# The bias of the folded linear layers: added to every row by GpSimd, or by a small matmul for each bin

## The reference, cut to what matters

```python
def gnn(x, edge_row, edge_col, W1, b1, W2, b2):
    agg = jax.ops.segment_sum(x[edge_col], edge_row, num_segments=6250)
    h = agg + x
    return (h @ W1 + b1) @ W2 + b2

x = x + gnn(layernorm(x), src, dst, ...)        # x: 6250 x 256, 100000 edges
x = x + experts(layernorm(x)[None], ...)[0]     # 8 experts, three layers each, weighted by a softmax
```

## Time and profile before

| | |
|---|---|
| median of 3 runs | 1579.49 us (1576.08 to 1580.27) |
| profiled execution | 1576.09 us, its span 1574.3 us |
| busy | PE 1236.1 us, DVE 1258.2, ACT 884.8, POOL 983.9 |
| first gather issued | 311.07 us from the span's start |
| last gather issued | 1410.40 us |

### The profile page before, as it was taken

One profiled execution on the slowest core, in us unless ns is written; L12 is line 12 of the kernel. 1 busy time (PEld: TensorE's weight loads), 2 busy tenths in 40 slices (PEclk: granted clock), 3 DMA queues, 4 the chain that ended last, 5 costly groups with the idle time before them and its releaser, 6 DMA issues.

```text
span 1574.3 us, 27908 instructions
## 1 busy us (share of the span) xinstructions
PE 1236.1 (79%) x7858; PEld 777.2 (49%) x7858; DVE 1258.2 (80%) x3421; ACT 884.8 (56%) x1593; POOL 983.9 (63%) x1001
## 2 busy tenths in 40 slices
PE   0035443554579999998999989999899999989996
PEld 0035332421235556565565656556565665645565
DVE  7999999864477888887888878988788888875655
ACT  6976656000054656665565655656556565656877
POOL 1140799177777777777777777777777777760000
PEclk9977655665699999999999999999999999999999
DMA  8020244043333343433434344343433434361000
GB/s 239 1 80 11 94 137 140 6 130 105 104 103 103 103 128 102 131 105 103 128 101 131 99 117 118 100 128 103 131 102 102 128 99 127 99 83 34 18 1 17
DMA packets 84072, 153.23 MB, mean 97 GB/s; under 512 B 18151, under 2 KB 56330, under 8 KB 83908
## 3 DMA queue, kind: packets, MB, share of 16 engines
q0 software_dynamic: 40608, 110.94, 25.5%
q1 hardware_dynamic: 43300, 40.36, 8.1%
HBM read 131.97 MB, written 19.27 MB: 96 GB/s over the span
## 4 chain that ended last, share of the span: by engine, by line
PE 45%; DVE 31%; issue 10%; DMA 6%; POOL 3%; DVEq 2%; ACT 2%; POOLq 0%; ACTq 0%; SPq 0%
PE PB L1318 10%; PE PA L1303 10%; PE PL L1335 9%; DVE zz L664 7%; DVE zz L665 6%; PE PN L1234 6%; DMA gbuf<-xn_hilo,dsti 6%; DVE acc L917 5%; PE PN L1235 4%; POOL gbuf L423 3%; DVE onehot L847 3%; PE PT L1259 3%; DVE xt L1023 1%; DVEq L900 1%; DVE zz L768 1%
## 5 line engine op out<-in xcount | busy, mean ns | idle before, releaser
L423 POOL DMA_INDIRECT gbuf<-xn_hilo,dsti x846 | 842.8, 996 | 291.2 <-issue 180.7
L917 DVE TENSOR_TENSOR acc<-acc,PN 128x256 f32 x798 | 331.6, 416 | 169.8 <-PE PN L1235 155.8
L1303 PE MATMUL PA<-yT,wsplit 128*128 128x512 f16 (+1 forms) x1248 | 290.8, 372 | 11.8 <-issue 11.8
L1335 PE MATMUL PL<-wsplit,h 128*128 128x256 f16 x2352 | 289.5, 273 | 11.3 <-DVE h L1008 4.2
L1318 PE MATMUL PB<-h,wsplit 128*128 128x512 f16 (+1 forms) x1248 | 284.7, 367 | 0.0
L557 ACT ACTIVATE h<-PA,bnt,bns 128x512 f16<-128x512 f32 (+1 forms) x208 | 156.6, 753 | 225.5 <-PE PA L1303 219.4
L1234 PE MATMUL PN<-gbuf,onehot 128*128 128x256 f16 x798 | 209.3, 283 | 83.5 <-DVE acc L917 44.7
L571 ACT ACTIVATE h<-PB,bnt,bns 128x512 f16<-128x512 f32 (+1 forms) x208 | 156.4, 752 | 203.9 <-PE PB L1318 199.5
L1335 PEld LDWEIGHTS PL<-wsplit,h 128*128 128x128 f16 x2352 | 227.9, 98 | 47.3 <-ACT zz L572 10.5
L1235 PE MATMUL PN<-gbuf,onehot 128*128 128x256 f16 x798 | 208.4, 282 | 0.0
L1234 PEld LDWEIGHTS PN<-gbuf,onehot 128*128 128x128 f16 x798 | 78.3, 98 | 233.9 <-DVE acc L917 122.1
(11 more groups left out here) (214 smaller groups left out, 1222.7 us busy)
## 6 DMA issues: line engine op xcount, KB each, us to landing
gbuf<-xn_hilo,dsti POOLq DMA_INDIRECT x846, 2.8
x_plus_bias<-xst SPq DMA_DIRECT2D x49, 128.0 KB, 1.7
xn_hilo<-onehot SPq DMA_DIRECT2D x49, 128.0 KB, 1.7
xt<-x_plus_bias SPq DMA_DIRECT2D x49, 128.0 KB
out<-xt SPq DMA_DIRECT2D x49, 128.0 KB
acc<-in_x SPq DMA_DIRECT2D x4, 1536.0 KB
h<-in_L_ffn_W SPq DMA_DIRECT2D x16, 256.0 KB, 2.8
h<-in_L_ffn_Wo SPq DMA_DIRECT2D x8, 256.0 KB, 2.7
```

Of the source, the lines that this page charges most:

```text
L423: pool.indirect_dma_start(gbuf[:, k % SLOTS, :], None, xn_dram, bass.IndirectOffsetOnAxis(dsti[:, k:k + 1], 0)).then_inc(gat[k % SLOTS], 16)
L917: V.tensor_tensor(to, to, bank[:, i, :], ALU.add).then_inc(s["acc_done"], 1)
L1303: last = T_.matmul(PA[:, h, 0:w], wsp[0][:, e, k, wp, h * P:(h + 1) * P], yT[:, par, yp, k, 0:w], start=n == 0, stop=n == 5)
L1335: last = T_.matmul(PL[:, i % 2, :], h2[:, e % 2, yp, k, i * P:(i + 1) * P], wsp[2][:, e, k, wp, :], start=n == 0, stop=n == 5)
```

## The change

x itself is stored to DRAM (`x_whole_bins`), by five transfers out of `acc` right after x is in, ahead of the loads of the layers' weights on SyncE's queue. The additions of b12 on GpSimd and the 49 stores of their results are gone; ScalarE's loop no longer waits for them, only once for the five stores. The bias is split into three f16 parts, one in each of three rows of `b3`, by six small instructions on ScalarE and GpSimd, with waits between them, and `linear` adds it to each bin's PSUM by a matmul of a 3-row `ones3` with `b3`. The loops of SyncE and GpSimd over the bins lose their lag of three.

```diff
+            sp.wait_ge(s["x_in"], 16 * 5)
+            for c in range(4):
+                sp.dma_start(x_dram[12 * c * P:(12 * c + 12) * P, :].rearrange("(t p) d -> p t d", p=P),
+                             acc[:, 12 * c:12 * c + 12, :]).then_inc(s["x_stored"], 16)
+            sp.dma_start(x_dram[(BINS - 1) * P:NPAD, :], acc[:, BINS - 1, :]).then_inc(s["x_stored"], 16)
             sp.dma_start(gw1, gW1.rearrange("(k p) n -> p k n", p=P)).then_inc(s["gnnw_in"], 16)
...
-            for t in range(BINS + LN_LAG):
-                if t < BINS:
-                    sp.wait_ge(s["xb_ready"], t + 1)
-                    sp.dma_start(xb_dram[t * P:(t + 1) * P, :], xst[:, t % 2, :]).then_inc(
-                        s["xst_stored" if t % 2 == 0 else "xst_stored1"], 16)
-                if t >= LN_LAG:
-                    u = t - LN_LAG
-                    sp.wait_ge(s["xnhi_ready"], u + 1)
-                    sp.wait_ge(s["xnlo_ready"], u + 1)
-                    sp.dma_start(xn_dram[u * P:(u + 1) * P, :], nst[:, u % 4, :]).then_inc(s[f"nst_stored{u % 4}"], 16)
+            for t in range(BINS):
+                sp.wait_ge(s["xnhi_ready"], t + 1)
+                sp.wait_ge(s["xnlo_ready"], t + 1)
+                sp.dma_start(xn_dram[t * P:(t + 1) * P, :], nst[:, t % 4, :]).then_inc(s[f"nst_stored{t % 4}"], 16)
...
+            pool.memset(ones3[:], 1.0).then_inc(s["b3_const"], 1)
+            for i in range(2):
+                pool.tensor_scalar(b3r[:, i:i + 1], bcol[0:3, :], i + 0.5, None, ALU.is_gt).then_inc(s["b3_const"], 1)
...
-            pool.wait_ge(s["b12_ready"], 1)
-            for t in range(BINS + LN_LAG):
-                if t < BINS:
-                    if t >= 2:
-                        pool.wait_ge(s["xst_stored" if t % 2 == 0 else "xst_stored1"], 16 * (t // 2))
-                    pool.tensor_tensor(xst[:, t % 2, :], acc[:, t, :], b12[:], ALU.add).then_inc(s["xb_ready"], 1)
...
+            pool.wait_ge(s["b3_high"], 1)
+            pool.tensor_tensor(b3w[:], b12[0:3, :], b3m[:], ALU.subtract).then_inc(s["b3_rest"], 1)
...
+            for t in range(BINS):
+                pool.wait_ge(s["xnhi_ready"], t + 1)
+                pool.tensor_tensor(nst[:, t % 4, D:2 * D], acc[:, t, :], nst[:, t % 4, 0:D],
+                                   ALU.subtract).then_inc(s["xnlo_ready"], 1)
             weights_low(range(W_FIRST, NW))
+            pool.wait_ge(s["b3_high"], 2)
+            pool.tensor_tensor(b3w[:], b3w[:], b3m[:], ALU.subtract).then_inc(s["b3_rest"], 1)
...
             nc.scalar.activation(b12[:], PL[:, 0, :], ACT.Copy).then_inc(s["b12_ready"], 1)
+            act.wait_ge(s["b12_ready"], 1)
+            act.wait_ge(s["b3_const"], 3)
+
+            def b3_high(values, i):
+                nc.scalar.activation(b3[:], values, ACT.Copy).then_inc(s["b3_part"], 1)
+                act.wait_ge(s["b3_part"], i + 1)
+                nc.scalar.activation(b3m[:], b3[:], ACT.Copy, scale=b3r[:, i:i + 1]).then_inc(s["b3_high"], 1)
+
+            b3_high(b12[0:3, :], 0)
...
+            act.wait_ge(s["b3_rest"], 1)
+            b3_high(b3w[:], 1)
             act.wait_ge(s["xnm_ready"], 1)
+            act.wait_ge(s["x_stored"], 16 * 5)
             for t in range(BINS):
-                act.wait_ge(s["xb_ready"], t + 1)
...
             weights_high(range(W_FIRST, NW))
+            act.wait_ge(s["b3_rest"], 2)
+            nc.scalar.activation(b3[:], b3w[:], ACT.Copy).then_inc(s["b3_part"], 1)
...
-                        last = T_.matmul(PT[:, i // 2, (i % 2) * D:(i % 2) * D + D], hT[:, k, i * P:(i + 1) * P],
-                                         W12[:, k, :], start=k == 0, stop=k == KD - 1)
+                        T_.matmul(PT[:, i // 2, (i % 2) * D:(i % 2) * D + D], hT[:, k, i * P:(i + 1) * P],
+                                  W12[:, k, :], start=k == 0, stop=False)
+                    last = T_.matmul(PT[:, i // 2, (i % 2) * D:(i % 2) * D + D], ones3[:], b3[:],
+                                     start=False, stop=True)
...
             chunk(C2, 0)
+            pe.wait_ge(s["b3_part"], 3)
```

More of the change, by code:

```diff
@@ L74, in build @@
     xn_dram = nc.dram_tensor("xn_hilo", (NPAD, 2 * D), F16, kind="Internal").ap()
-    xb_dram = nc.dram_tensor("x_plus_bias", (NPAD, D), F32, kind="Internal").ap()
+    x_dram = nc.dram_tensor("x_whole_bins", (NPAD, D), F32, kind="Internal").ap()
     with ExitStack() as ctx:
@@ L100, in build @@
         b12 = sb("b12", [P, D], F32)
+        b3w = sb("b3w", [3, D], F32)
+        b3m = sb("b3m", [3, D], F32)
+        b3 = sb("b3", [3, D], F16)
+        b3r = sb("b3r", [3, 2], F32)
+        ones3 = sb("ones3", [3, P], F16)
         bosb = sb("bosb", [3 * EX, D], F32)
@@ L132, in build @@
         lowrow = sb("lowrow", [3 * EX, 2], F32)
-        xst = sb("xst", [P, 2, D], F32)
+        bolow = sb("bolow", [3 * EX, D], F32)
         junk = sb("junk", [P, EF], F16)
@@ L206, in build @@
             "srcf_ready", "counted", "x_summed", "nmean_ready", "x_squared", "var_ready", "xsd_ready", "xrs_ready",
-            "xnm_ready", "xb_ready", "xn_ready", "xnhi_ready", "xnlo_ready", "xst_stored", "nst_stored0", "nst_stored1",
-            "nst_stored2", "nst_stored3", "xst_stored1", "whi_ready", "wlo_ready",
-            "prep_pe", "prep_dve", "prep_act", "firsts", "first_ready", "prep_own", "bn_sqrt", "sched_dve", "sched_pe", "b12_ready",
+            "xnm_ready", "x_stored", "xn_ready", "xnhi_ready", "xnlo_ready", "nst_stored0", "nst_stored1",
+            "nst_stored2", "nst_stored3", "whi_ready", "wlo_ready",
+            "prep_pe", "prep_dve", "prep_act", "firsts", "first_ready", "prep_own", "bn_sqrt", "sched_dve", "sched_pe", "b12_ready", "b3_const", "b3_part", "b3_high", "b3_rest",
             "oh_ready", "select", "own", "nmr_ready", "max_ready", "bo_split", "ent_done", "acc_done",
@@ L298, in load_x @@
                 for i in range(T):
-                    sp.dma_start(xt[:, par, i, :], xb_dram[bass.ds(b[i] * P, P), :]).then_inc(s[f"xt_in{par}"], 16)
+                    sp.dma_start(xt[:, par, i, :], x_dram[bass.ds(b[i] * P, P), :]).then_inc(s[f"xt_in{par}"], 16)
             def store(g, T, par):
@@ L372, in bias @@
                 pool.wait_ge(s["bo_split"], split[0])
-            high, low = nst[0:3 * EX, 2, 0:D], xst[0:3 * EX, 0, :]
+            high, low = nst[0:3 * EX, 2, 0:D], bolow[:]
             pool.wait_ge(s["small_in"], 16 * 16)
@@ L394, in _ @@
             weights_low(range(W_FIRST))
-            pool.wait_ge(s["b12_ready"], 1)
-            for t in range(BINS + LN_LAG):
-                if t < BINS:
-                    if t >= 2:
-                        pool.wait_ge(s["xst_stored" if t % 2 == 0 else "xst_stored1"], 16 * (t // 2))
-                    pool.tensor_tensor(xst[:, t % 2, :], acc[:, t, :], b12[:], ALU.add).then_inc(s["xb_ready"], 1)
[L402 to L408, removed]
-                    pool.tensor_tensor(nst[:, u % 4, D:2 * D], acc[:, u, :], nst[:, u % 4, 0:D],
-                                       ALU.subtract).then_inc(s["xnlo_ready"], 1)
+            pool.wait_ge(s["b3_high"], 1)
+            pool.tensor_tensor(b3w[:], b12[0:3, :], b3m[:], ALU.subtract).then_inc(s["b3_rest"], 1)
+            pool.wait_ge(s["xrs_ready"], 1)
+            pool.wait_ge(s["nmean_ready"], 1)
+            pool.tensor_tensor(xnm[:], nmean[:], xrs[:], ALU.mult).then_inc(s["xnm_ready"], 1)
+            for t in range(BINS):
+                pool.wait_ge(s["xnhi_ready"], t + 1)
+                pool.tensor_tensor(nst[:, t % 4, D:2 * D], acc[:, t, :], nst[:, t % 4, 0:D],
+                                   ALU.subtract).then_inc(s["xnlo_ready"], 1)
             weights_low(range(W_FIRST, NW))
+            pool.wait_ge(s["b3_high"], 2)
+            pool.tensor_tensor(b3w[:], b3w[:], b3m[:], ALU.subtract).then_inc(s["b3_rest"], 1)
             for i in range(4):
@@ L1417 @@
 WARM_N = 10
-LN_LAG = 3
 PASSES = [(0, 0), (0, 1), (1, 0)]
```

3 lines of the change are left out of this document (1 added, 2 removed).

## The result

The changed kernel takes 1566.07 us (median of 5 runs, 1564.3 to 1568.6), the kernel before 1576.1 us on the same chip (1575.86 to 1580.27). The ratio is 0.9929, with a 95% interval from 0.9915 to 0.9944: 11 us faster by the ratio, 10 by the medians. The forecast was 1562.3 us, 17.2 us under the median of the first three runs, 1579.49. The profiled execution took 1564.3 us, its span 1562.4 us against 1574.3: 11.9 us less.

What follows compares the result with a forecast made beforehand. Bound: VectorE's sort, GpSimd's 1100 us gather stream, a tail of some 150 us. Savings 13.5 + 3.6 + 0.8 - 0.7 = 17.2 us against the median 1579.49 gave 1562.3 us; eight in ten between 1556 and 1571.

Steps and rivals of the forecast that it cites:

- The sort: VectorE's part up to 311 us: fewer contended GpSimd instructions, at 0.44 us each; weight pieces at 0.90 us.
- these three terms: Before the gathers: additions gone save 13.5 us, weight pieces moved 3.6, additions before the loop against ScalarE's small instructions 0.8.
- The rival of whole-instruction collisions (B): VectorE's sort: each contended GpSimd instruction costs 0.73 us, saving 22.6 instead of 13.5 us; 1553 us, chance 0.10.
- The first gather: Start of GpSimd's gathers after the sort: at 294 us instead of 311, the last 17 us sooner as well.
- SyncE's queue: Stores of x ahead of the small loads: 21.6 us to issue, small loads in at 64.8 us, nothing lost.
- The stream of gathers: GpSimd from 311.07 to 1410.40 us: 846 gathers at 1.30 us each, without a pause, unchanged.
- Rival C: GpSimd's gathers 0.01 to 0.02 us slower each, 8 to 17 us, eating the gain; 1575 to 1580 us, chance 0.07.
- The 49 matmuls: Bias matmuls on TensorE: 5.9 us by 1384 us covered by waits for gathers, 0.7 us lost after.
- I take 0.135: Price of one bias matmul on TensorE, 0.135 us, from four expert bias matmuls 24 rows deep taking 0.61 us.
- the bound of 0.15: Upper price of a bias matmul on TensorE, 0.15 us: 49 cost 7.4 us if nothing covers them.
- The condition that the forecast named for losing the cover: Gathers: cover goes if TensorE's lag fills the 18 slots and stops GpSimd; 5.9 us are under five gathers.
- rival A: TensorE's added bias matmuls all show: 17.9 - 7.4 = 10.5 us saved, 1569 us, chance 0.13.

Runs made afterwards that it cites:

- dead additions: Changed kernel plus 49 GpSimd additions of two SBUF operands in its loop, results never read: 1582.79 us, ratio 1.0056 to the kernel before.
- the memsets: Changed kernel plus 49 GpSimd memsets in its loop, writing 128x256 f32 that nothing reads: 1565.29 us, one run.
- The kernel with the matmuls alone: Kernel before plus 49 three-row matmuls of zeros, nothing removed: ratios 1.0102 and 1.0105 on two slower chips (1808.89 and 1809.75 us).
- The doubled stores: Changed kernel with the five stores of x done first to a spare tensor: 1792.73 us, one run, against 1791.38 for the kernel before.
- the kernel of 128 rows: Changed kernel, bias matmul filled to 128 rows, 125 of them zero: 1556.63 us, one run; on a slower chip 1782.85 us, ratio 0.9949.

## Why the prediction was right, and which term was wrong

**The sort: right in mechanism and size.** Forecast 13.5 + 3.6 + 0.8 = 17.9 us. VectorE reached the copy `hT<-PT` (L725 before, L741 now), which has all of the contention behind it, at 260.15 us and before at 277.65: 17.5 us. Of contention it had 16.8 us left in the loop and 6.8 in the weight pieces, where the forecast had 16.7 and 7.2. The reciprocal came 0.6 us sooner, not 0.8, with a wait of 1.2 us instead of under 1. By these three terms it would have been 18.0 us. The total is 17.5 because of two things that the forecast didn't have: VectorE caught up with TensorE and waited 1.5 us more for it than before (above all the 2.04 us at 246.02), and short instructions of the schedule gave about 1.0 back. Put back as dead additions, they cost the 17.9 us again. The rival of whole-instruction collisions (B) falls: 9 us more would have been gained. The Trainium skill ("SBUF — State Buffer", Who interferes with whom) also says that a GpSimd instruction that only writes doesn't contend with VectorE's two-operand ones; the memsets' 0 us agree.

**The first gather: 15.9 us sooner, not 17.** Behind VectorE's last turn TensorE's 16 small matmuls took 3.60 us, not 1.96. Before and after:

```profile
307.50 1.96 PE L1214 MATMUL PL<-junk,zz 128*128 128x18 f32 x16 [0.61 <-DVE zz L665]
```

```profile
289.99 3.60 PE L1230 MATMUL PL<-junk,zz 128*128 128x18 f32 x16 [0.62 <-DVE zz L681]
```

Its granted clock was 0.50 there (1.2 GHz) and 1.00 (2.4 GHz) before, after the same 10.6 us of idle time and the same 20 matmuls, which ran at 0.50 to 0.52 in both. Of the other twelve executions profiled, nine had 1.96 or 1.97 us and three 3.60. The kernel with the matmuls alone had 1.96 on one chip and 3.60 on the other, so this isn't a matter of the change.

**SyncE's queue: right that it costs nothing.** The stores waited until 31.5 us for x, not 28.2, but issued in 14.8 us, not 21.6, so the small loads came at 58.8 us, not 64.8. That full rings hold up the issuing is an inference of the prediction; the rows show how long it took and that the DMA engines were at full share meanwhile. The doubled stores show the cover as forecast: 18.5 us later at the small loads, and a first gather no later than without. VectorE's wait for the root is 2.6 us there in place of 1.2, but it is 2.8 to 3.0 us in six executions without doubled stores too, so nothing of it can be put down to them. It goes with an earlier wait of ScalarE for TensorE, at the copy of W12: 8.8 us there, 8.0 to 8.4 in those six, and 6.3 in the changed kernel.

**The stream of gathers: right.** 1392.42 - 295.21 = 1097.2 us against 1099.3. Rival C has nothing to show.

**The 49 matmuls: the wrong term.** The step that failed is "I take 0.135", and with it the bound of 0.15. It measured 0.38 us: 0.11 for the matmul and 0.27 for coming from 128 rows and going back. The nearest rows were four shallow matmuls in a row. Start to start they take 1424.96 - 1424.42 = 0.54 us, which is the 0.135 each; but that is one alternation spread over four, and what stands ahead of the first falls outside it. The same trace had it in the row of the weight loads, which the prediction didn't read:

```profile
1424.42 0.33 PEld L1291 LDWEIGHTS PT<-bo,wT 24*128 24x128 f16 x4 [0.42 <-issue]
1424.96 1.21 PEld L1335 LDWEIGHTS PL<-wsplit,h 128*128 128x128 f16 x12 [0.21 <-issue]
```

The loads stand on both sides there as well. The Trainium skill ("TensorEngine Tiling (Array Packing)", Key Properties) says: "Changing tiling mode (not just tile) drains the TensorE". If three rows count as another mode than 128, this is it; the rows agree, with 0.33 us of standing in f16 and in f32 at 3 rows, and 0.21 to 0.42 at 24 rows. The page gives no time for it, and no run here shows matmuls of 50 to 127 rows.

From this the rest follows. Through eleven groups TensorE had 11 x 1.53 = 16.8 us more to do, not 5.9, and the cover was the 7.8 us near the end and smaller waits for gathers between 320 and 500 us, which went from 29.4 to 21.9 us. The condition that the forecast named for losing the cover, a lag that stops GpSimd, came true at 1108 us and three more places. What was left over shows in the tail: 6.1 us, of which 1.53 + 0.31 = 1.8 are group 11 and the last bin, and the other 4.3 the lag at the last gather. The steps of 3.90, 4.09, 4.39 and 4.99 us fit the depth of the cover: eleven groups of 0.44 or 0.63 us stay under 7.8 us, and the tail is 163.0 and 164.2; eleven of 0.93 go beyond, and it is 168.7.

So rival A's place was right, that TensorE's additions show, with 10.5 us saved; 11.9 us were. But it came about at another price: 18.7 us added and 6.1 (by the tail of the profiled executions) to 8.5 (by the medians) of them seen, not 7.4 added and all seen. The forecast kept its direction and stayed within its range since the large term was right. That the time itself was missed by only 3.8 us is in part luck: with two more runs the median of the kernel before came down from 1579.49 to 1576.1 us, and the forecast saving of 17.2 us from there gives 1558.9, 7.2 us under the 1566.07 measured.

## What to carry to other kernels

Price a matmul with what it stands next to, not by itself: where the depth of the contraction changed between neighbours here (3 or 24 rows against 128), the weight load stood until TensorE was nearly through with what was ahead. Keep shallow matmuls together, put one wide one ahead of the deep ones, or fill them up with rows of zeros. Read the row of the weight loads too when a matmul is priced from a trace. And ask of every cover how many microseconds it is deep: the same matmuls that were covered in part here cost their full price, 18 to 19 us, on two other chips.

## What the runs showed of the hardware

A weight load of 3 rows behind matmuls of 128 rows stands 0.33 us, in f32 as in f16; the whole round trip costs 0.27 to 0.30 us in f16 and 0.36 in f32. A bias matmul of three f16 rows costs 0.38 us alternating, 0.11 behind another such. Filled up to 128 rows it costs 0.11. Loads of 24 rows stand 0.21 us behind matmuls of 256 columns.

49 memsets of 128x256 on GpSimd (0.31 us each) cost VectorE's SBUF-to-SBUF instructions nothing, 49 additions 17.9 us by the first gather.

TensorE had either clock at the same place in kernels that differ nowhere near it, which is worth 1.6 us. And on two chips the kernel before took 14% longer than on the others, while TensorE's and VectorE's busy times in the kernel of 128 rows differed by 1% and less (PE 1250 us against 1238, DVE 1237 against 1240); the added waits are put down to something unresolved, and what it is stays open.
